# Fused attention and expert kernel: the order of one layer's last attention block, and of exponentials and row norms in each block

## The reference, cut to what matters

```python
def attention(x):                       # 16 heads of 32 values, one decay for each head
    q, k, v = split(x @ w_qkv)
    q, k = elu(q) + 1, elu(k) + 1       # = min(exp(z), 1) + relu(z)
    running_kv   = scan(s = decay * s + k * v)
    running_ksum = scan(s = decay * s + k)
    den = clip(sum_over_head(q * running_ksum), 1e-6)
    return (q * running_kv / den) @ w_out

x = x + attention(layernorm(x))
h = layernorm(x)
shared = (silu(h @ sw_gate) * (h @ sw_up)) @ sw_down          # 704 wide, for all tokens
routed = top 2 of 8 experts by softmax(h @ gate_w), each 352 wide
x = x + shared + routed
```

## Time and profile before

| | |
|---|---|
| median of three executions | 714.49 us (713.29 to 715.10) |
| the profiled execution's own time | 715.02 us |
| its span, first to last instruction | 713.2 us |
| busy: PE (TensorE) / DVE (VectorE) / ACT (ScalarE) / POOL (GpSimd) | 93% / 60% / 36% / 32% |
| mean granted TensorE clock | 0.972 of full |
| attention, to the last block's first shared product | about 0 to 237 us |
| last block's outputs, with the first shared units | about 237 to 280 us |
| shared units, then routed jobs | about 280 to 700 us |

### The profile page before, as it was taken

One profiled execution on the slowest core, in us unless ns is written; L12 is line 12 of the kernel. 1 busy time (PEld: TensorE's weight loads), 2 busy tenths in 40 slices (PEclk: granted clock), 3 DMA queues, 4 the chain that ended last, 5 costly groups with the idle time before them and its releaser, 6 DMA issues.

```text
span 713.2 us, 11766 instructions
## 1 busy us (share of the span) xinstructions
PE 663.0 (93%) x3797; PEld 432.7 (61%) x3798; DVE 426.6 (60%) x746; ACT 257.1 (36%) x397; POOL 231.0 (32%) x269
## 2 busy tenths in 40 slices
PE   7868999899989989899999899999999999999992
PEld 6646677578657465556565465665656565656561
DVE  7757996997987753677787777633333333333331
ACT  5336263354342343546665665421111111111110
POOL 6201121322101313334343254124444444444431
PEclk9999999989989899999999999999999999999997
DMA  6561003513422497897564433268777777777753
GB/s 222 174 231 31 16 16 88 160 48 89 107 71 74 109 256 156 213 229 183 146 171 121 95 46 67 47 117 132 132 132 132 132 132 132 132 135 132 133 89 42
DMA packets 111236, 86.89 MB, mean 122 GB/s; under 512 B 79280, under 2 KB 86448, under 8 KB 111200
## 3 DMA queue, kind: packets, MB, share of 16 engines
q1 hardware_dynamic: 88848, 43.94, 25.7%
q0 software_dynamic: 12272, 27.34, 22.6%
q10 hardware_dynamic: 10080, 15.14, 6.8%
HBM read 44.45 MB, written 23.33 MB: 95 GB/s over the span
## 4 chain that ended last, share of the span: by engine, by line
PE 69%; DVE 8%; issue 2%; ACT 2%; DMA 1%; POOL 1%; ACTq 1%; SPq 0%; POOLq 0%; DVEq 0%
PE ps_y L514 17%; PE ps_g L514 16%; PE ps_u L514 15%; PE ring L389 14%; PE turn_h L534 3%; DVE routed L1409 1%; ACTq L373 1%; PE ps_norm L401 1%; DMA out_dram<-y_job,job_tok 1%; PE ps_den L450 1%; PE ring L476 0%; DMA xg_odd<-xn_hl 0%; DVE den L1304 0%; ACT xn L1040 0%; POOL squares L952 0%
## 5 line engine op out<-in xcount | busy, mean ns | idle before, releaser
L1349 DVE TENSOR_TENSOR hidT<-turn_h,hidT 128x384 f16<-128x384 f32 x71 | 39.5, 556 | 112.0 <-ACT hidT L1096 109.8
L945 POOL DMA_INDIRECT out_dram<-y_job,job_tok x39 | 61.9, 1586 | 109.1 <-DVE y_job L1683 102.2
L1092 ACT ACTIVATE silu<-ps_g,job_silu 128x352 f32<-128x352 f32 x39 | 21.6, 553 | 189.5 <-PE ps_g L514 158.9
L389 PE MATMUL ring<-xnT_h,wq_h 128*128 128x512 f32 x192 | 82.0, 427 | 7.5 <-DVE wq_l L1248 2.5
L514 PE MATMUL ps_y<-routed,hidT 128*128 x351 | 82.1, 379 | 1.3 <-DVE hidT L1349 1.3
L855 POOL TENSOR_SCALAR var_eps<-mean_var 128x1 f32<-128x1 f32 x32 | 12.9, 402 | 203.4 <-DVE mean_var L1339 114.9
L389 PE MATMUL ring<-xnT_l,wq_h 128*128 128x512 f32 x192 | 78.6, 410 | 0.0
L389 PE MATMUL ring<-xnT_h,wq_l 128*128 128x512 f32 x192 | 78.3, 408 | 0.0
L514 PE MATMUL ps_g<-routed,x_in 128*128 x468 | 76.4, 313 | 0.0
L514 PE MATMUL ps_u<-routed,x_in 128*128 x468 | 76.2, 313 | 0.0
L952 POOL TENSOR_TENSOR squares<-squares 128x704 bf16<-128x704 bf16 (+1 forms) x24 | 42.3, 1761 | 93.1 <-ACT squares L1060 93.1
(11 more groups left out here) (232 smaller groups left out, 1108.7 us busy)
## 6 DMA issues: line engine op xcount, KB each, us to landing
routed<-in_L_ffn_w_gate_dram ACTq DMA_DIRECT2D x7, 704.0 KB, 4.8
routed<-in_L_ffn_w_up_dram ACTq DMA_DIRECT2D x7, 704.0 KB, 7.7
x_res<-in_L_attn_x_dram SPq DMA_DIRECT2D x18, 256.0 KB, 3.2
out_dram<-x SPq DMA_DIRECT2D x16, 256.0 KB, 3.3
xn_scratch<-xn_hl SPq DMA_DIRECT2D x16, 256.0 KB, 2.4
out_dram<-y_job POOLq DMA_DIRECT2D x16, 256.0 KB, 4.2
x_in<-in_L_attn_x_dram SPq DMA_DIRECT2D x14, 256.0 KB, 2.7
routed<-in_L_ffn_w_down_dram ACTq DMA_DIRECT2D x7, 512.0 KB, 8.9
```

Source lines behind the costliest of these rows:

```text
L389: ins = pe.matmul(ps, a, b, start=(i == 0), stop=(i == len(steps) - 1))
L945: pool.indirect_dma_start(out[:, :], bass.IndirectOffsetOnAxis(job_tok[:, r:r + 1], 0), y_job[:, b, :], None, compute_op=ALU.add).then_inc ...
L1092: act.activation(silu[:, :], ps_g[:, 0:F], ACT.Silu, scale=by).then_inc(s["silu_s"], 1)
L1349: dve.tensor_tensor(hidT[:, 1], turn_h[:, 0:FC, :], hidT[:, 0], ALU.subtract).then_inc(s["hidT_s"], 1)
```

## The change

Nothing is computed differently; the order changes, and three banks change places.

- TensorE: in the last block, the output product of tile 12 waits for the remainder of each chunk, not for all four; `turn_hidden(0)` stands ahead of `output` of tile 14, and `gate(10)` behind it. The banks of chunks and tiles 1, 2, 3 are ring 2, ring 4, ring 1 (were 1, 2, 4); `ps_y` moves to the bank of ring 2.
- VectorE: `residual(10)` is no longer ahead of `denominators(3)`. `residual` is split into the sum and the statistics. The order is: denominators, sums of tiles 10 and 11, then divisions and remainders that alternate by chunk, with the statistics of tile 10, `hidden(0)` and later the statistics of tile 11 between them.
- ScalarE: the last block's roundings stand ahead of the norms of tiles 10 and 11; the third SiLU stands behind the norm of tile 14. In every block from 1 on, `phi_parts(n, 1, 0)` comes ahead of `rows_before(3, 2)` and of `piece_step(n * KC)`.
- GpSimd: the load of expert 0 stands ahead of `rstd_2` of tiles 10 and 11.

```diff
 PSUM: ps_y and ps_free change places
@@ TensorE
-            last_banks = [(turn..., None), (ring[1], 1), (ring[2], 2), (ring[4], 4)]
+            last_banks = [(turn..., None), (ring[2], 2), (ring[4], 4), (ring[1], 1)]
             def output(n, j):
-                pe.wait_ge(s["al_s"], (n + 1) * KC)
+                by_chunk = n == NB - 1 and j == 0       # split_product then waits for al_s,
+                if not by_chunk:                        # n * KC + k + 1 ahead of chunk k
+                    pe.wait_ge(s["al_s"], (n + 1) * KC)
...
             output(NB - 1, 1)
-            gate(before_last + 2)
-            output(NB - 1, 2)
             pe.wait_ge(s["x2_s"], last + 1)
             turn_hidden(0, True)
+            output(NB - 1, 2)
+            gate(before_last + 2)
             output(NB - 1, 3)
@@ GpSimd
             for n in range(NB + 2):
+                if n == NB:
+                    (wait for all projections, memset, load_expert(pool, 0))
                 for t in (2, 3):
                     if n >= 2:
                         rstd_2((n - 2) * TPB + t)
...
-                if n == NB:
-                    (the same)
@@ ScalarE, every block
                 carry_states(n, 0)
+                if n == 0:
+                    piece_step(0)
+                phi_parts(n, 1, 0)
                 rows_before(3, 2)
-                piece_step(n * KC)
-                phi_parts(n, 1, 0)
+                if n:
+                    piece_step(n * KC)
@@ ScalarE, last block
             gate_silu(0, shared_by, True)
+            hi_a(NB - 1, 0)
+            hi_a(NB - 1, 1)
+            gate_silu(1, shared_by)
+            hi_a(NB - 1, 2)
+            hi_a(NB - 1, 3)
             rows_2(before_last + 2)
-            gate_silu(1, shared_by)
             rows_2(before_last + 3)
-            for c in chunks:
-                hi_a(NB - 1, c)
+            upper_hidT(0)
             rows_2(last)
-            upper_hidT(0)
             rows_2(last + 1)
+            rows_2(last + 2)
             gate_silu(2, shared_by)
-            rows_2(last + 2)
@@ VectorE, end of each block
-                tile_before(residual, 2)
+                if n < NB - 1:
+                    tile_before(residual, 2)
@@ VectorE, last block (t = tile 8)
             denominators(NB - 1)
+            residual_sum(t + 2)
+            residual_sum(t + 3)
+            divide_chunk(NB - 1, 0)
+            residual_stats(t + 2)
+            divide_chunk(NB - 1, 1)
             hidden(0, shared_by, True)
-            residual(t + 3)
+            lo_a_chunk(NB - 1, 0)
+            divide_chunk(NB - 1, 2)
+            lo_a_chunk(NB - 1, 1)
+            divide_chunk(NB - 1, 3)
+            lo_a_chunk(NB - 1, 2)
+            lo_a_chunk(NB - 1, 3)
+            residual_stats(t + 3)
             lo_2(t + 2)
-            divide(NB - 1)
-            lo_a(NB - 1)
+            residual(t + 4)
             lo_2(t + 3)
-            residual(t + 4)
             residual(t + 5)
-            lo_2(t + 4)
             hidden(1, shared_by)
             rest_hidT(0)
+            lo_2(t + 4)
             residual(t + 6)
             lo_2(t + 5)
             residual(t + 7)
+            lo_2(t + 6)
             rest_hidT(1)
-            lo_2(t + 6)
             lo_2(t + 7)
             hidden(2, shared_by)
```

More of the change, by code:

```diff
@@ L237, in preln_decay_attention_moe @@
         ps_g = psum("ps_g", [P, 512], stack=pm)
+        psum("ps_free", [P, 512], stack=pm)
         ps_y = psum("ps_y", [P, D], stack=pm)
-        psum("ps_free", [P, 512], stack=pm)
         ps_u = psum("ps_u", [P, 512], stack=pm)
@@ L382, in _, with split_product @@
         def _(pe):
-            def split_product(ps, pairs):
+            def split_product(ps, pairs, ready=None):
                 steps = []
@@ L388, in split_product @@
                 for i, (a, b) in enumerate(steps):
+                    if ready is not None and i % 3 == 0:
+                        pe.wait_ge(s["al_s"], ready + i // 3 + 1)
                     ins = pe.matmul(ps, a, b, start=(i == 0), stop=(i == len(steps) - 1))
@@ L451, in sum_heads @@
                               start=True, stop=True, tile_position=(0, DH * cc)).then_inc(s["den_mm"], 1)
-            last_banks = [(turn[:, :, :].rearrange("p k q -> p (k q)"), None), (ring[1], 1), (ring[2], 2), (ring[4], 4)]
+            last_banks = [(turn[:, :, :].rearrange("p k q -> p (k q)"), None), (ring[2], 2), (ring[4], 4), (ring[1], 1)]
             def last_bank(c, freed_by, value):
@@ L489, in output @@
                 split_product(ps[:, :], [((at_h[:, k, tok], at_l[:, n % 2, k, tok]), (wo_h[:, k, :], wo_l[:, k, :]))
-                                         for k in chunks]).then_inc(s["out_mm"], 1)
+                                         for k in chunks], n * KC if by_chunk else None).then_inc(s["out_mm"], 1)
             def gate(t):
@@ L893, in _ @@
             for n in range(NB + 2):
+                if n == NB:
+                    for name in ("k_mm", "v_mm", "q_mm"):
+                        pool.wait_ge(s[name], NB * KC)
+                    pool.memset(routed_raw[0:OVER, 0, DOWN_AT + (FC - 1) * D:EXPERT], 0.0).then_inc(s["over_0"], 1)
+                    load_expert(pool, 0)
                 for t in (2, 3):
@@ L1306, in last_bank, with divide_chunk, lo_a_chunk, residual_sum @@
             def last_bank(c):
-                return (turn[:, :, :].rearrange("p k q -> p (k q)"), ring[1][:, :], ring[2][:, :], ring[4][:, :])[c]
+                return (turn[:, :, :].rearrange("p k q -> p (k q)"), ring[2][:, :], ring[4][:, :], ring[1][:, :])[c]
+            def divide_chunk(n, c):
+                i = n * KC + c
+                dve.wait_ge(s["ex_mm"], i + 1)
+                dve.wait_ge(s["num_s"], i + 1)
+                a = num[:, n % 2, c, :]
+                by = last_bank(c) if n == NB - 1 else ring[items[(n, c, "ex")] % RING][:, :]
+                dve.tensor_tensor(a, a, by, ALU.mult).then_inc(s["a_s"], 1)
+            def lo_a_chunk(n, c):
+                i = n * KC + c
+                dve.wait_ge(s["ah_s"], i + 1)
+                a = num[:, n % 2, c, :]
+                dve.tensor_tensor(at_l[:, n % 2, c, :], a, at_h[:, c, :].bitcast(F32), ALU.subtract)\
+                    .then_inc(s["al_s"], 1)
             def divide(n):
                 for c in chunks:
[L1311 to L1315, removed]
+                    divide_chunk(n, c)
             def lo_a(n):
                 for c in chunks:
[L1319 to L1325, removed]
+                    lo_a_chunk(n, c)
+            def residual_sum(t):
                 b = t % 2
@@ L1335, in residual, with residual_stats @@
                     .then_inc(s["x2_s"], 1)
+            def residual_stats(t):
+                b = t % 2
                 dve.wait_ge(s["x2_s"], t + 1)
@@ L1339, in residual @@
                 dve.bn_aggr(mean_var2[:, b, :], stats2[:, b, :]).then_inc(s["var2"], 1)
+            def residual(t):
+                residual_sum(t)
+                residual_stats(t)
             def lo_2(t):
```

## The result

The changed kernel takes **703.31 us** (median of 4 executions, 701.87 to 705.68) against 714.16 us (4 executions) of the kernel before in the same measurement: ratio 0.984, 95% interval 0.981 to 0.987. Forecast: 702.4 us, range 697.5 to 707.5. The profiled execution took 705.68 us, 2.4 above the median, with a span of 703.9 us; before it was 715.02 and 713.2. So the two profiles differ by 9.3 us, less than the medians do.

What follows compares the result with a forecast made beforehand. TensorE, busy 663.0 of 713.2 us, was taken as the bound, so only its idle or slow stretches could be won. Terms -6.6 - 1.1 + 1.0 - 5.4 = -12.1 us gave 702.4 us on the median's scale, range 697.5 to 707.5.

Steps and rivals of the forecast that it cites:

- Part 1: Block 3: chunk 1's exponential ahead of the norm starts the Q product 4.7 us earlier, clock gives 2.3; -6.6 us.
- The late division: Block 3, VectorE: the first division, which frees the bank of the product after, comes 0.4 us too late.
- Part 2: Block 2: exponential ahead of the norm, TensorE then waits for `run_kv` until 140.5; -1.1 us, clock gain taken as 0.
- Part 3: Block 1: the weight piece's square moves behind the exponential and delays VectorE's fold; costs +1.0 us, no clock fall taken.
- Part 4: Last block: waits and low clock removed -8.9, put back 1.1, new SyncE-queue waits 1.5 and 0.9; -5.4 us.
- Part 5: Expert 0's load issued 13 us earlier on GpSimd, off the transfers of tiles 11 to 13; 0 in the sum.
- Everything behind `gate(15)` as one piece: After the last gate: work is released in fixed order and moves together; wrong if its time changes by over 1.5 us.
- (i): Block 1: the clock falls behind the longer idle time, +2.5 us, 704.9 us; alone 0.2.
- (ii): Block 2: the clock stays up, -2.7 us, 699.7 us; alone 0.25.
- the tail gives back its gain: Last block gains 0 to 1 instead of 5.4 us, VectorE's alternation or SyncE-chain landings being later; 707.5 us, chance 0.1.
- the load collides with it: Last block: expert 0's load lasts beside the stores of tiles 10 to 13; +16, 718.5 us, chance 0.03.
- The tail without new waits: Last block: SyncE's chain hides and the 2.4 us of new waits vanish; 700.0 us, chance 0.08.

Runs made afterwards that it cites:

- second profile: The changed kernel profiled once more with no edit, in a later measurement: 703.50 us, ratio 0.985, span 699.7 us.
- first profile: The changed kernel's original profile against the kernel before: profiled execution 705.68 us, span 703.9 us; median 703.31 us.
- the kept order: The changed kernel, but in block 1 ScalarE squares the weight piece ahead of chunk 1's exponential, as before: 703.14 us, ratio 0.984.
- fillers: Small unused matmuls behind the expansions of blocks 1 to 3, added to the changed kernel with block 1's old order and stores ahead of turns: 699.09 us, ratio 0.979.
- the kernel with the stores first: The changed kernel with SyncE's store of tile t+1 ahead of the turn of tile t, tiles 10 to 15: 702.01 us, ratio 0.983.

## Why the prediction was right, and where it wasn't

The forecast missed the median by 0.9 us, and most of the waits that it named went or came where it said. That it was so close is in part luck. Its case, a clock that stays up in block 1 and falls in block 2, is in neither profile: the first has both falls, the second none. From A to `gate(15)`, all that the change touches, the two profiles gained 11.4 and 12.7 us (206.43 less 194.99 and 193.78), where the sum had 12.1, and some terms were off against each other.

- **Part 1 (-6.6): right in kind, -5.9.** The Q product of block 3 starts 1.65 us behind the first expansion in both profiles (196.75 to 198.40 in the first), and 5.91 before (195.15 to 201.06): 4.2 us earlier (forecast 4.7). The rest of the -6.6 of the table's fourth row, 2.4 in the second profile, is block 2's clock. The step that was too early is "so VectorE is ready at 199.13 - 4.14 = 195.0": it waits 0.33 us for its own `num` ahead of the states, and TensorE, whose expansions are done at 197.9, waits 0.51 us for `run_kv`. The clock stayed at 1.00, as forecast. To the last `ps_u` another 1.7 (2.3 of clock less 0.4 of the division forecast, 1.9). The late division is there, 0.29 us.
- **Part 2 (-1.1): -1.0** to block 2's Q product. The clock, put at 0 with up to -2.7 open, gave 2.4 in the second profile and 1.2 in the first. From block 2's Q product to block 3's first expansion it is 53.48 us before, 51.12 in the second and 52.25 in the first profile: even where the clock falls, the low stretch costs half as much as before. The step that failed is "I take 0 in the sum": between a clock that stays up and the fall of before there was a third case, a smaller fall.
- **Part 3 (+1.0): +0.9.** Measured by the kept order. The fall was priced at +2.5 and costs 1.6 in block 1 (56.88 less 55.32).
- **Part 4 (-5.4): -5.7 and -4.2** in the two profiles. The reciprocal's wait 0.3 (0.4), `gate(12)` 1.2 and 1.0 (1.5), clock 1.00 to the first output, and from the first expansion to the first output 5.99 us (forecast about 6). Inside these, two errors cancel: the eight expansions took 2.2 us up to `ps_g`, not 1.5, and the waits of 0.2 for ring 1 and 0.5 for `hidden(0)` didn't come. What came otherwise is a wait of 1.2 and 1.1 us at `gate(13)`: the turned tile of the first profile took 5.61 us to land, not the 3.40 of the earlier trace rows. The 0.9 us at `down_product(1)` did not come in the first profile and was 1.65 in the second, so the new waits of SyncE's chain sum to 2.4 and 3.7 us, with 2.4 forecast. In the kernel with only the last block changed the part is -2.4, with a fall of the clock behind that same wait. That the clock stays up in the last block holds in both profiles of the changed kernel, then, and not in each with this order.
- **Part 5 (0): wrong as a term by itself.** Put back, the load costs 5.7 us by the medians and 4.4 to 5.9 by the segment. "The data then come before 248 instead of up to 259, which takes them off the transfers of tiles 11 to 13" was right (it was issued from 229.75 us on and the last piece landed some 7 us after its issue at 232 us), but the short landings that part 4 counts on were bought by it; the cost was hidden in that part's price, and "0 in the sum" holds only with the load moved.
- **Everything behind `gate(15)` as one piece:** 433.6 and 431.2 against 432.8 us. The first is within the 1.5 us set; the second is 1.6 us less and just outside. It is the one profile of the three without a fall of the clock behind the norm's wait (0.83 from 290 to 300 us in the first, 0.86 from 300 to 312 us before). `gate(15)` came 10.05 us earlier in the first profile, just inside the 10 us set, with a start that was 1.4 us later; the second has 11.9.
- **The difference of the two profiles, -9.3 us,** is +1.4 (start to A, untouched code), +0.9 and +1.6 (block 1, wait and fall), -1.0 and -1.2 (block 2), -5.9 (block 3), -5.7 (last block) and +0.7 behind `gate(15)`, but for rounding. The start ranges over 73.9 to 76.9 us in all kernels of the study; with it goes the clock before block 1 (from 50 to 60 and 60 to 70 us 0.89 and 1.00 before, at 73.97 us, 0.73 and 0.83 with block 1 kept, at 76.89 us).

**The rivals.** The clock's two cases both occurred, (i) in 3 of 6 and (ii) in 4 of 10 profiles with the new order of that block and no fillers. The Trainium skill (TensorE: Matmul & The Clock Gate, "What's actually happening") says that the monitor runs freely and the point of change varies from run to run; one program with and without falls (0.57 and 1.00 at 88 us) agrees. That the tail gives back its gain, with residuals late by their landings, and that the load collides with it is what the kernel with the load put back shows: landings of 8.3 us, though a loss of 5.7 and not of 16 us. The tail without new waits is what the kernel with the stores first has in its profile.

## What to carry to other kernels

When a turn that waits for a result and a store that frees a buffer share one queue, put the store first: it was worth 2.6 to 4.1 us of the segment here (in single profiles; the median shows it only together with block 1's order), while waiting by chunk was worth nothing at the last gate as long as the queue's order stood. Price a large load's place by the landings of the small transfers on the chain, not by its own due time: a term of "0" can be the condition of another. Compare segments of two or three profiles between fixed points before a difference of 1 or 2 us is explained; the untouched start alone ranged over 3 us.

## What was not expected of the hardware

- The clock fell behind expansion matmuls (32 rows) with only 1.6 to 2.0 us of idle time, in about half of the profiles, and one program had it in one profile and not in the other. A fall cost about 2.4 us with the old order of block 2, 1.1 to 1.2 us with the new one and 1.6 us in block 1.
- Beside a 2.1 MB load on GpSimd's queue not only the landings grew (8.3 us) but, once, the issue of a transposing DMA on SyncE, from 1.23 to 4.05 us, and everything behind it on that queue was later.
- Keeping the clock up with fillers in the blocks moved the median by nothing that can be told.
- ScalarE is held by its own DMA issues. Its timeline in the changed kernel, behind `gate(15)`:

```profile
285.80 3.00 ACTq L373 DMA_DIRECT2D routed<-in_L_ffn_w_down_dram  x2
288.85 1.38 ACT L1064 ACTIVATE squares<-routed 128x1408 bf16<-128x1408 f32 x1 [7.48 <-issue]
```

The square waited 7.48 us for the eight issues of the loads of experts 1 and 2, of which the last two are shown, and TensorE's 3.4 us wait hangs on it.
